# Feed-forward rows normalised two steps ahead, the first scores of the second attention layer moved into the last feed-forward steps, and 16 late residual sums moved from VectorE to GpSimd

## What is computed

```python
x = x + _L0_xattn_ref(_layernorm(x, axis=-1), ctx_2048, ...)   # banded attention, 8 heads, gated by ctx
x = x + _L0_ffn_ref(_layernorm(x, axis=-1), ...)
x = x + _L1_xattn_ref(_layernorm(x, axis=-1), ctx_2048, ...)   # full attention, 8 heads, rotary q and k
x = x + _L1_ffn_ref(_layernorm(x, axis=-1), ...)               # 256 -> 1024 -> 256

# _L0_ffn_ref
out = jnp.einsum('bln,nk->blk', x, weight) * scale
v_norm = jnp.maximum(jnp.linalg.norm(out, axis=-1, keepdims=True), EPS)
scaled_norm = sqrt_c * v_norm
out = out * (jnp.tanh(scaled_norm) / (scaled_norm + EPS))
o_norm = jnp.maximum(jnp.linalg.norm(out, axis=-1, keepdims=True), EPS)
out = out * jnp.minimum(max_norm / o_norm, 1.0)
```

## Time and profile before

| | |
|---|---|
| median of 3 runs | 1329.06 us (1322.9 to 1331.28) |
| profiled execution | 1333.56 us |
| its span, first to last instruction | 1331.8 us |
| mean granted TensorE clock in the span | 0.982 of full speed |
| first attention layer, with feed-forward steps 0 to 7 | up to about 533 us |
| feed-forward steps 8 to 35 | about 534 to 592 us |
| iteration -1 of the second layer | about 592 to 606 us |
| iterations 0 to 31 | about 606 to 1100 us |
| second feed-forward block | to the end |

### The profile page before, as it was taken

The page is one execution under the profiler, slowest core; times in us unless marked ns, Lnnn a source line. Parts: engine busy times, 40 slices in busy tenths (PEclk is TensorE's granted clock), DMA queues, the critical chain, the costliest instruction groups (busy, mean ns, idle before and its releaser), DMA issues.

```text
span 1331.8 us, 35495 instructions
## 1 busy us (share of the span) xinstructions
PE 1263.2 (95%) x11100; PEld 839.9 (63%) x11100; DVE 909.1 (68%) x1924; ACT 847.8 (64%) x1849; POOL 676.6 (51%) x1169
## 2 busy tenths in 40 slices
PE   6999999999999998778899999999999989999998
PEld 3666667667776765454565656666666546666665
DVE  6778778888887875569999978888888842111110
ACT  2567677776777776556888788888888763222111
POOL 4577778787878865045455445555555211000000
PEclk9999999999999999888999999999999999999999
DMA  8554454544444440034344434444444300000000
GB/s 206 120 131 107 114 117 111 116 110 118 113 114 117 99 92 7 13 67 102 89 107 96 97 90 103 105 112 97 103 108 108 86 2 16 16 16 16 16 16 32
DMA packets 90486, 113.34 MB, mean 85 GB/s; under 512 B 13971, under 2 KB 80275, under 8 KB 82739
## 3 DMA queue, kind: packets, MB, share of 16 engines
q1 hardware_dynamic: 89216, 111.25, 35.9%
q10 hardware_dynamic: 1206, 1.29, 0.3%
HBM read 18.66 MB, written 4.19 MB: 17 GB/s over the span
## 4 chain that ended last, share of the span: by engine, by line
PE 73%; DVE 10%; POOL 6%; issue 4%; ACT 3%; DMA 2%; SPq 1%; POOLq 0%; ACTq 0%; DVEq 0%
PE bank L491 13%; PE bank L451 12%; PE bank L467 12%; PE bank L721 8%; PE bank L712 8%; PE bank L449 5%; DVE row_max L1157 5%; PE bank L503 4%; POOL probs L1386 4%; PE bank L672 2%; PE bank L522 2%; PE bank L555 2%; PE bank L532 1%; PE bank L543 1%; DVE stats L1029 1%
## 5 line engine op out<-in xcount | busy, mean ns | idle before, releaser
L1157 DVE TENSOR_REDUCE row_max<-bank 128x2 f32<-128x384 f32 (+1 forms) x1024 | 598.5, 617 | 107.0 <-PE bank L451 102.8
L757 ACT ACTIVATE probs<-bank 128x384 f32<-128x384 f32 (+1 forms) x1024 | 536.8, 542 | 165.1 <-PE bank L467 154.8
L451 PE MATMUL bank<-Ks,Qs 96*128 96x192 bf16 (+1 forms) x2048 | 371.4, 263 | 10.9 <-DVE row_max L1157 9.7
L467 PE MATMUL bank<-Qs,Ks 128*128 128x192 bf16 (+1 forms) x2048 | 366.3, 261 | 13.9 <-ACT probs L757 11.1
L1386 POOL TENSOR_SCALAR_AFFINE_SELECT probs<-probs 128x256 f32<-128x256 f32 (+1 forms) x512 | 259.1, 530 | 105.9 <-ACT probs L757 85.5
L451 PEld LDWEIGHTS bank<-Ks,Qs 96*128 96x128 bf16 x2048 | 186.4, 98 | 121.1 <-DVE row_max L1157 39.7
L491 PE MATMUL bank<-probs,V 128*32 128x192 f32 (+1 forms) x4096 | 248.0, 360 | 4.7 <-POOL probs L1386 3.4
L467 PEld LDWEIGHTS bank<-Qs,Ks 128*128 128x128 bf16 x2048 | 186.7, 98 | 45.4 <-ACT probs L757 28.7
L449 PE MATMUL bank<-band,ident 128*128 128x384 bf16 x512 | 168.8, 330 | 2.5 <-DMA Ks<-Ks 2.0
L491 PEld LDWEIGHTS bank<-probs,V 128*32 128x32 f32 x4096 | 107.3, 109 | 84.5 <-issue 40.5
L1323 DVE TENSOR_TENSOR X<-bank,X 128x256 f32 (+1 forms) x32 | 13.6, 425 | 185.6 <-PE bank L721 185.6
(11 more groups left out here) (114 smaller groups left out, 1625.2 us busy)
## 6 DMA issues: line engine op xcount, KB each, us to landing
Ks<-Ks SPq DMA_DIRECT2D x64, 576.0 KB
Qs<-Qs SPq DMA_DIRECT2D x128, 192.0 KB
Qs<-Qp SPq DMA_DIRECT2D x192, 64.0 KB
Ks<-Kp SPq DMA_DIRECT2D x192, 64.0 KB
X<-in_x SPq DMA_DIRECT2D x4, 1024.0 KB, 13.8
side<-in_ctx_crossed SPq DMA_DIRECT2D x32, 128.0 KB, 2.1
side<-in_ctx SPq DMA_DIRECT2D x32, 128.0 KB, 2.1
out<-X SPq DMA_DIRECT2D x8, 512.0 KB, 3.0
```

The costliest lines, as they stand in the source:

```text
L451: last = nc.tensor.matmul(dst[:, blk * win:(blk + 1) * win], Qs[0:SHIFT_ROW, pair[1], h, blk * P:(blk + 1) * P], Ks[0:SHIFT_ROW, pair[1], ...
L467: last = nc.tensor.matmul(dst[:, blk * win:(blk + 1) * win], Ks[:, pair[1], h, blk * P:(blk + 1) * P], Qs[:, pair[1], h, start(blk):start( ...
L757: nc.scalar.activation(probs[:, h % 8, 0:2 * win], exp_bank[h % 2][:, 0:2 * win], ACT.Exp, scale=SCALE).then_inc(s["exped"], 1)
L1157: nc.vector.tensor_reduce(row_max[:, pair[1], h // HEADS, 0, h % HEADS * 2:h % HEADS * 2 + 2], bank_of(pair, h)[:, 0:2 * win].rearrange("p ...
```

## The change

Five edits, and the constants FF0_AHEAD = 2 and FF0_LATE = 28:

1. In `ff0` on VectorE, step n normalises row n + 2 instead of row n; step 0 does rows 0, 1 and 2. To fit, the reciprocal for rows 28 to 31 moves from n = 28 to n = 26, and ScalarE's root for it from n = 25 to n = 23.
2. From step 28 on the transposes use bank 2 alone and the products banks 3 and 4 alone, so that banks 0, 1 and 5 are free. A product then waits until the one two steps before has been copied out.
3. Iteration -1 starts inside the feed-forward steps: TensorE does its slots 0 to 2 ahead of step 32 and 3 and 4 ahead of step 33, the other eleven after step 35; VectorE does slots 0 and 1 ahead of step 33, 2 to 4 ahead of 34, 5 to 7 ahead of 35, and the rest after. ScalarE does the iteration after its last step, with the hyperbolic tangent of the gains between slots 8 and 9. The gains move to h = 8 and h = 14.
4. The 16 late sums are computed by GpSimd in iterations 2 to 9, as two instructions each: `ff * gain` in place, then `X + ff`. The statistics stay on VectorE, at h = 6 and h = 14, and wait for GpSimd's second instruction.
5. GpSimd's twelve first iterations are written out instead of looped.

```diff
--- before.py
+++ after.py
@@ -32,2 +32,4 @@
 FF0_LAG = (2, 2, 4)
+FF0_LATE = 28
+FF0_AHEAD = 2
 FIRST_CHUNK, SECOND_CHUNK = 6, 16
@@ -283,2 +286,4 @@
 
+            if n >= FF0_LATE:
+                return bank[2], n
             return bank[2 if n > FILL and n % 2 else 0], n if n <= FILL else n - 1
@@ -289,2 +294,4 @@
                 return bank[(1, 5)[n % 2]], n - 1
+            if n >= FF0_LATE:
+                return bank[(3, 4)[n % 2]], n - 1
             return bank[(1, 5, 3, 4)[n % 4]], n - 1 if n < FILL + 2 else n - FF0_RING + 1
@@ -688,6 +695,13 @@
                     iteration(*early(-2, range(6, HPP)))
+                if n == 32:
+                    e.wait_ge(f_xTs, FF0_LATE)
+                    e.wait_ge(f_keep, FF0_LATE - 2)
+                    iteration(*early(-1, range(0, 3)))
+                if n == 33:
+                    iteration(*early(-1, range(3, 5)))
 
             ff0_steps(ff0, between)
+            iteration(*early(-1, range(5, HPP)))
             e.wait_ge(f_keep, PAIRS)
-            run(-1)
+            run(0)
             tail = next_tail
@@ -976,3 +990,3 @@
                     iteration(*early(-2, range(0, 6)))
-                if n == 25:
+                if n == 23:
                     e.wait_ge(ln_var, 5)
@@ -984,4 +998,6 @@
             root(1, FIRST_CHUNK, PAIRS)
+            iteration(*early(-1, range(0, 9)))
             tanh(1, FIRST_CHUNK, PAIRS)
-            run(-1, loop_from=4)
+            iteration(*early(-1, range(9, HPP)))
+            run(0, loop_from=4)
             tail = next_tail
@@ -1074,2 +1090,7 @@
             e.wait_ge(f_upd, n + 1)
+            vector_stats(e, n, ff_vec)
+
+        def late_stats(e, n):
+
+            e.wait_ge(late_upd, 2 * (n - SECOND_CHUNK) + 2)
             vector_stats(e, n, ff_vec)
@@ -1107,5 +1128,5 @@
 
-            if n == -1 and h == 2:
+            if n == -1 and h == 8:
                 gain_norm(e, 1, FIRST_CHUNK, PAIRS)
-            if n == -1 and h == 6:
+            if n == -1 and h == 14:
                 gain_clip(e, 1, FIRST_CHUNK, PAIRS)
@@ -1117,4 +1138,4 @@
                 vector_rstd(e, 6, FIRST_CHUNK, SECOND_CHUNK)
-            if 2 <= n < 10 and h in (3, 11):
-                ff0_update(e, SECOND_CHUNK + 2 * (n - 2) + h // 8)
+            if 2 <= n < 10 and h in (6, 14):
+                late_stats(e, SECOND_CHUNK + 2 * (n - 2) + h // 8)
             if n == 9 and h == 15:
@@ -1219,5 +1240,5 @@
 
-            def iteration(r):
+            def iteration(r, heads=range(HPP)):
                 p1, p3, m1 = at(r, 1), at(r, AHEAD), at(r, -1)
-                for h in range(HPP):
+                for h in heads:
                     if within and isinstance(r[0], int):
@@ -1265,8 +1286,9 @@
             def ff0(pair):
-                n, u = num(pair, FF0_RING), pair[1]
+                n = num(pair, FF0_RING)
                 if n == 0:
                     e.wait_ge(ffn_ready, PREP_BLOCKS)
-                if active(pair, FF0_RING):
-                    wait_some(e, f_xT, n - FF0_RING + 1)
-                    vector_apply(n, ff0_xn[:, u, :], f_xn)
+                for step in range(FF0_AHEAD + 1) if n == 0 else (n + FF0_AHEAD,):
+                    if step < PAIRS:
+                        wait_some(e, f_xT, step - FF0_RING + 1)
+                        vector_apply(step, ff0_xn[:, step % FF0_RING, :], f_xn)
                 late = at(pair, -FF0_LAG[2], FF0_RING)
@@ -1303,3 +1325,3 @@
                     vector_var(e, TAIL_NORM, PAIRS, ln_vec, PAIRS + NORM_STEPS)
-                if n == 28:
+                if n == TAIL_NORM - FF0_AHEAD:
                     vector_rstd(e, 5, TAIL_NORM, PAIRS)
@@ -1307,6 +1329,13 @@
                     iteration(*early(-2)[:1])
+                if n == 33:
+                    iteration(*early(-1, range(0, 2)))
+                if n == 34:
+                    iteration(*early(-1, range(2, 5)))
+                if n == 35:
+                    iteration(*early(-1, range(5, 8)))
 
             ff0_steps(ff0, between)
+            iteration(*early(-1, range(8, HPP)))
             e.wait_ge(f_keep, PAIRS)
-            run(-1, loop_from=4)
+            run(0, loop_from=4)
             tail = next_tail
@@ -1411,2 +1440,16 @@
                                         ALU.mult).then_inc(s["gated"], 1)
+
+            def late_update(n):
+
+                e.wait_ge(f_step, 8 * 2)
+                nc.gpsimd.tensor_scalar(ff[:, n, :], ff[:, n, :], gain[:, n:n + 1], None,
+                                        ALU.mult).then_inc(late_upd, 1)
+                wait_apart(e, (late_upd, 2 * (n - SECOND_CHUNK) + 1))
+                nc.gpsimd.tensor_tensor(X[:, n, :], X[:, n, :], ff[:, n, :], ALU.add).then_inc(late_upd, 1)
+
+            def late_updates(r, part):
+
+                n = num(r) if isinstance(r[0], int) else -1
+                if 2 <= n < 10:
+                    late_update(SECOND_CHUNK + 2 * (n - 2) + part)
 
@@ -1425,2 +1468,3 @@
                 else:
+                    late_updates(r, 0)
                     rot_sum("A", "q", p3, 0, q_rest)
@@ -1429,2 +1473,3 @@
                     split_max(e, nc.gpsimd, s, l, p1, 0)
+                    late_updates(r, 1)
                     split("k", p3, Kp, k_rest, "k_mid", "k_parts")
@@ -1432,3 +1477,3 @@
 
-            iterations(e, iteration, extra and (lambda n: extra(e, n)), last=(l == 0))
+            iterations(e, iteration, extra and (lambda n: extra(e, n)), last=(l == 0), loop_from=(1, 4)[l])
```

More of the change, by code:

```diff
@@ L213, in build @@
         f_upd = sem("f_upd")
+        late_upd = sem("late_upd")
         g_xn = sem("g_xn")
```

## The result

| | before | changed |
|---|---|---|
| median of 4 runs each | 1330.17 us (1322.9 to 1333.28) | 1313.12 us (1310.68 to 1317.0) |
| ratio | | 0.9878, interval 0.9846 to 0.9911 |
| profiled execution | 1333.56 us | 1310.68 us |
| its span | 1331.8 us | 1309.0 us |

The kernel is 17 us faster by the medians. Its first row is the time from the start of the span, each other row the distance between two starts in the timelines, and an iteration ends with the split of the maxima after h = 15.

A forecast was written before the change was run, and what follows sets the result against it. TensorE, busy 95% of the span, was taken as the bound, with VectorE holding it up in the changed stretches. 12.2 + 6.0 = 18.2 us off the profiled 1333.56 gives 1315.4, or 1311 from the 1329.06 median; range 1302 to 1322.

The forecast's parts named there:

- A1: Feed-forward step 11 to the second layer's first projection (n = 18): normalising two ahead removes VectorE's tail waits; 8.2 us gained.
- A2: Steps 18 to 22: with rows 20 and 21 ready, TensorE works through its wait before step 20; 4.3 us gained.
- A3: Pair 0's stack, asked for at step 32: arrives 15.8 us behind the split, TensorE waits 3.5; first score 17.0 us earlier.
- A4: Iteration -1: copies, a new wait for pair 2's turn and low-clock products give back 4.8 us.
- VectorE's wait for the turn: Iteration -1: pair 2's turn at h = 2 stands ahead of head 3's maximum on VectorE; about 2 us.
- Part B: Iterations 2 to 9: two sums per iteration leave VectorE, making TensorE the bound again; 6.0 us gained.
- The late sums do not pay: Rival, iterations 2 to 9: GpSimd is late at h = 14 and VectorE waits as long; 1317 us, chance 0.20.
- The seam pays half: Rival, feed-forward steps and iteration -1: ScalarE bounds or the low clock stays, gain 6; 1317 us, chance 0.20.
- part A: Feed-forward steps through iteration -1: 17.0 - 4.8 = 12.2 us gained, bounds 3.5 and 17.5.
- Normalising ahead does not do what it says: Rival, feed-forward steps: TensorE next waits for a bank not yet copied out; total gain 9, 1320 us, chance 0.08.
- Slower, VectorE waits for GpSimd 16 times: Rival, iterations 2 to 9: waits of 1.2 us each eat both parts; 1339 us at 1.8 each, chance 0.07.
- a stack later than 17 us behind pair 0's split: Sign of being wrong, before the first score: the stack was forecast 15.8 us behind the split.

The follow-up runs named there:

- e3: The kernel before with only rows normalised two steps ahead (four banks, iteration -1 after step 35): 1313.14 us, ratio 0.9883.
- e2: The kernel before with only the late sums on GpSimd and GpSimd's loop written out: 1323.79 us, ratio 0.9952.
- the square: Four kernels on one chip, scores early or after step 35, late sums on GpSimd or VectorE: 1311.85, 1309.54, 1315.6 and 1314.68 us.
- e5: The changed kernel with the second layer's row normalisation at h = 5 instead of h = 6: 1311.09 us, ratio 0.9873.
- e1: The changed kernel with the late sums back on VectorE and GpSimd's loop as before: 1317.8 us, ratio 0.992.
- e7: The changed kernel with iteration -1 after step 35, row normalisation at h = 5 and first `gain_clip` before step 12, not 11: 1308.42 us, ratio 0.9863.
- changed_third: The changed kernel run once more, unaltered, in the third group: 1311.85 us, ratio 0.987.
- e9: The kernel before with only rows normalised two ahead and the new bank assignment: 1314.68 us, ratio 0.9888.
- changed_again: The changed kernel run once more, unaltered, in the second group: 1313.94 us, ratio 0.9892.

## Why the prediction was right, and where its terms were off

- **The forecast**: 1311 us, measured 1313.12 and, in the later groups, 1313.94 and 1311.85. The mechanism is the one forecast: TensorE no longer waits for the row, and with the waits the low clock behind them goes.
- **A1 and A2** (8.2 and 4.3) measured 8.0 and 4.3. Following VectorE through its own queue, and not TensorE's waits, gave that. The 8.0 are in part luck: in six other profiles with edit 1 the clock falls behind TensorE's wait of 2.5 us in step 11, and A1 is 6.4. The prediction had no such wait at step 11. What the sum lacked is that normalising ahead also helps the steps before n = 11: 2.9 us in the profiled pair, and 21.3 us for these steps in all twelve profiles with edit 1 against 24.2 in the two without. Edit 1 alone shows the path: against the profiled kernel before, e3 has 2.9, 6.4 and 4.3 us in these lines and 3.4 in A3, and it is 15.6 us faster by the medians.
- **A3**: TensorE's wait for the stack was put at 3.5 us and is 3.18. The stack came 17.0 us behind the split and not 15.8. Of the 1.2 us, 0.4 are the transfer itself: the prediction put 5.6 us from its issue to the drained queues, and in every profile with a wait for the stack the score starts 6.0 us behind the issue. The other 0.8 us are that the last transfer is issued later behind the split (11.0 against 10.2 us). GpSimd's split of pair 0 takes 5.2 instead of 4.7 us there, but that is not the whole cause: in e2 it takes 4.7 and the issue still comes after 10.8. What sets it stays open. The gain of this line is not edit 3's, as e3 shows.
- **A4** (4.8 given back) is 4.2, and 1.1 of it comes back in iteration 0. The size was near, by parts that were not: VectorE's wait for the turn is 3.98 us where about 2 were forecast. And the term was read wrongly: the prediction counted 17.0 - 4.8 as what the early scores bring together with the steps. It never set them against iteration -1 left behind step 35. There the first score would be at the same time, since the stack sets it, and the 4.8 would not be paid. With a wait of 3.5 us for the stack already in the sum, this could have been read off: whoever must wait for a DMA gains nothing by asking earlier.
- **Part B** (6.0) is 4.0 in the profiled pair and 4.4 by the square. The term was mis-sized: the prediction took TensorE to be the bound again and left one collision out of the sum, which it had named itself. The row takes 0.91 instead of 0.41 us beside `k_rest` and 0.40 at h = 5; the extra 0.50 us are less than the 0.73 of the GpSimd instruction and than the 0.85 that the prediction allowed for. The Trainium skill ("SBUF — State Buffer", section "Who interferes with whom") says that a tensor_scalar of VectorE in a 2-port mode contends with GpSimd for a shared pair of ports: the one issued first has it for its whole instruction and the other is fully blocked. The runs agree that the two collide, but not on the size: the row loses less than the length of `k_rest`, and by the profile it starts first. Which mode it ran in no run shows. It is not GpSimd's added work that it meets but `k_rest`, into which the moved statistics push it; that is read off the order of the rows, while e5 shows the collision itself. Of the 0.5 us, 0.3 reaches each of the iterations 3 to 8. GpSimd's own terms held: 0.93 + 0.73 us for a sum where 0.85 + 0.73 were taken, 11.36 us busy where 11.7 were.
- **The rivals.** *The late sums do not pay*: 4.4 us, refuted by e1, e2 and the square. *The seam pays half*: part A is 11.5 us, and 12.6 with iteration 0. *Normalising ahead does not do what it says*: its mechanism, a bank not yet copied out, is there, once and for 2.5 us; e7 takes it away, for 0.7 us and a steadier clock. *Slower, VectorE waits for GpSimd 16 times*: no wait of VectorE for a sum of GpSimd's stands in its list over iterations 3 to 8.
- **The sum.** The profile before lay 3.4 us above its median and the one after 2.4 below. So the 22.8 us of the profiles are 17 in the medians. In the profiled pair the terms of the sum make 15.6 us where 18.2 were forecast, and 7.1 us lie in lines without a term: 2.9 in the steps before n = 11 and 1.1 in iteration 0, which come again in the changed kernel's other two profiles, and 1.3 ahead of step 0 and 1.8 in iteration 10, which vary from profile to profile. That 18.2 came out so near the 17 of the medians is in part luck: what B and A3 had too much is about what the steps before n = 11 and iteration 0 had too little.
- **The signs.** One sign of being wrong was a stack later than 17 us behind pair 0's split. The first score is 17.0 us behind it in the profile after and 17.3 in changed_third, so this sign is met, by a little. VectorE's wait for the turn is twice the one forecast. Iterations 3 to 8 are 15.0 us apart and not 14.7 to 14.8. The row's wait, TensorE's wait for the stack and the absence of a wait for GpSimd's sums are as forecast.

## What to carry to other kernels

Before work is moved ahead of a wait, ask what ends that wait: if it is a transfer with its own chain, moving the asker earlier gives nothing, and everything queued behind it is late. When an operation is handed to GpSimd, look at each VectorE instruction whose neighbour on GpSimd changes, not only at the one that left; here one row in the wrong place took 0.3 us of the 0.8 that an iteration could have gained, and moving it by one slot made another collision in iteration -1. And after a queue is reordered, read the first wait that took the old one's place: a single `gain_clip` ahead of a copy held TensorE for 2.5 us, which cost 0.7 us at the full clock and 2.3 when the clock fell behind it.

## What the runs showed of the hardware

Iteration 10 takes 16.4 to 16.7 us in some profiled executions and 18.2 to 18.4 in others (once 19.56, in e9), of the same kernel too. Windows view of it in the kernel before and in the changed one:

```profile
766.40:784.79 18.39, 15.77 (x143) 10.18 (x142) 13.26 (x25) 14.92 (x31) 8.01 (x15) 0.91 0.36 84
```

```profile
745.55:762.13 16.58, 14.11 (x143) 9.03 (x143) 13.15 (x25) 14.49 (x31) 8.05 (x14) 1.00 0.40 93
```

In both TensorE waits once, 2.6 and 2.4 us, for ScalarE (`probs`), and behind that wait the granted clock falls to the lower level of 1.2 GHz in the one and stays at 2.4 in the other. The length of the wait does not decide it: changed_third has 2.6 us there and no fall (16.71 us, clock 1.00), changed_again 2.6 us and a fall (18.17 us, 0.91). Iteration 2 does the same behind a wait of 1.8 us (17.60 us at 0.90 in changed_again, 16.26 at 1.00 in the first profile), and so does the stretch behind step 11: of eleven profiles with a wait of 2.51 to 2.53 us there, six have the fall and five have not. In the changed kernel's own three profiles a fall costs 1.3 us in iteration 2 and 1.5 to 1.6 in the other two places. The first profile had none of the three. What decides a fall these runs don't show.

The second surprise is that GpSimd can be slower beside VectorE as well: its `Qp<-q_rest` of pair 0 takes 1.16 us at 556.93 in the changed kernel, beside a row of VectorE's normalised rows and copies, where it takes 0.85 us elsewhere (570.05, 599.41). The rows beside it keep their 0.40 us.
